# Last edge layer's table of query rows: one scatter of a four-row record a column in place of three, and pair gathers that start one row further on

## Chip, cores and metric

The kernel runs on one core of a Trainium2 chip. The metric is the device time of one launch in microseconds (us); the median of the runs counts.

## What is computed

Four layers on 6250 nodes of 256 features: a graph attention layer, a mixture of experts, a second graph attention layer with edge attributes, and a slice attention. The change is in the third. Its reference, cut to what matters (H = 8 heads of C = 32, 100000 edges sorted by target):

```python
q = (x @ Wq + bq).reshape(n, H, C)
k = (x @ Wk + bk).reshape(n, H, C)
v = (x @ Wv + bv).reshape(n, H, C)
e = (edge_attr @ We).reshape(-1, H, C)
k_j = k[src] + e
v_j = v[src] + e
q_i = q[dst]
alpha = jnp.sum(q_i * k_j, axis=-1) / jnp.sqrt(jnp.float32(C))
amax = jax.ops.segment_max(alpha, dst, num_segments=n)
ex = jnp.exp(alpha - amax[dst])
alpha = ex / denom[dst]
out = jax.ops.segment_sum(v_j * alpha[:, :, None], dst, num_segments=n)
out = out.reshape(n, HC) + x @ Ws + bs
```

`q_i = q[dst]` needs one row of q for each edge. Since the edges are sorted by target, two neighbouring edges need either the same row twice, or the rows of two targets that follow one another among the targets that have edges (their ranks).

## The kernel before

The program is a row of stages (`build`), each a block in which every engine has its own instruction list; a stage ends when all five engines have finished it, a barrier passes, its semaphores are cleared, and a second barrier passes. Two stages matter here, with an empty one between them.

**`layer1_tables` (L2000 to L2257).** Nodes lie on 128 partitions, 49 columns each, handled in 7 groups of 7 columns. For a group VectorE normalizes 7 columns (`normalize_group`), TensorE turns them (L2228) and ScalarE copies them out of PSUM (L2194); for a column TensorE makes query, key, value and skip rows in eight matmuls of 512 columns (L2246), VectorE adds the biases in four instructions (L2170 to L2173), and ScalarE writes the scaled query row twice side by side into the tile `twice` (L2212). GpSimd (POOL) then scatters it into the table `c.q` in HBM, in which a target of rank r owns the four rows 4r+1 to 4r+4:

```python
pool.indirect_dma_start(pairs, at_slot(0, i), twice[...], None)          # 2 KB: rows 4r+2 and 4r+3
for n in range(1, 3):
    pool.indirect_dma_start(c.q, at_slot(n, i), twice[:, g % 2, j, 0, :], None)   # 1 KB each: rows 4r+4 and 4r+1
```

So 3 scatters a column, 147 in all. The first and last row of the table, which no target owns, are zeroed by SyncE (SP, L2045 and L2046). The 28 gathers at L2067, ahead of the scatters in POOL's list, fetch expert outputs of the last 14 columns, which VectorE adds during group 0. Where groups meet, VectorE adds the skip rows to x (L2180, 2 us) and normalizes the group after the next, ahead of its first bias addition; TensorE can do two columns meanwhile, since the PSUM tile `psO` has two buffers. Buffers of `qrow` and `twice` come free over `q_free` and `twice_free`; the latter needs all scatters of the group before to be issued and those of two groups before to be landed. When all groups are done, VectorE marks the segments of the edges and makes `c.q_of`, the pair index of each two edges (`segments_of_edges`, L2137 to L2152). SP stores the key and value rows of each group (L2052), and the stage waits for all stores and scatters.

**`order_attributes`** sorts edge attributes where edges come unsorted. Here they come sorted; every engine only passes its barriers, and POOL and SP read a flag and jump.

**`edge_pass` (L1023 to L1252).** 98 blocks of 8 edges on 128 partitions. For a block POOL issues 8 gathers of key and value rows (L1111, 2 KB a partition) and 4 gathers of query pairs (L1118, 2 KB), SP loads edge attributes (L1077, L1078) and stores the states (L1084). TensorE turns the attributes and adds keys (L1239, L1249, L1250). VectorE forms the products, the maxima, the weights and a running sum, in a fixed chain of instructions a block (L1140 to L1176). Queries, keys, values and attributes have two buffers.

Of the kernel before, what the change touches and what calls it, by code (L numbers as in the profile page):

```python
# [6 lines left out]
I32 = mybir.dt.int32  # L7
ALU = mybir.AluOpType
# [3 lines left out]
P = 128  # L12
N, D = 6250, 256
# [5 lines left out]
T = 784  # L19
# [1006 lines left out]
def edge_pass(c):  # L1026
# [8 lines left out]
    with ExitStack() as s:  # L1035
# [66 lines left out]
        def _(pool):  # L1102
            pairs = c.q.rearrange("(r two) d -> r (two d)", two=2)
            for blk in range(NBLK):
# [11 lines left out]
                for m in range(B // 2):  # L1116
                    t = blk * B + 2 * m
                    pool.indirect_dma_start(q[:, u, m, :], None, pairs, bass.IndirectOffsetOnAxis(  # L1118
                        ap=c.q_of[:, t // 2:t // 2 + 1], axis=0)).then_inc(gq[u], 16)
# [879 lines left out]
def layer1_tables(c):  # L1999
# [5 lines left out]
    with ExitStack() as s:  # L2005
# [6 lines left out]
        start, slots = sb("start", [P, NI], I32), sb("slots", [P, 3, NI], I32)  # L2012
# [3 lines left out]
        qrow, kvrow, srow = sb("qrow", [P, 2, GT, D]), sb("kvrow", [P, 2, GT, 2 * D]), sb("srow", [P, GT, D])  # L2016
        twice = sb("twice", [P, 2, GT, 2, D])
# [4 lines left out]
        starts_in, counted, summed, slots_made, numbered, twice_free, sc0, sc1, ends_in, turned = (sem(n) for n in (  # L2022
            "starts_in", "counted", "summed", "slots_made", "numbered", "twice_free", "sc0", "sc1", "ends_in", "turned"))
        q_biased, q_copied, q_free = sem("q_biased"), sem("q_copied"), sem("q_free")
# [6 lines left out]
        picked = [twice[:, 1], kvrow[:, 1].rearrange("p j (r d) -> p j r d", r=2)]  # L2031
# [3 lines left out]
        def _(sp):  # L2035
# [9 lines left out]
            sp.dma_start(c.q[0:1, :], c.zrow[0:1, 0:D]).then_inc(ends_in, 16)  # L2045
            sp.dma_start(c.q[4 * NI * P + 1:4 * NI * P + 2, :], c.zrow[0:1, 0:D]).then_inc(ends_in, 16)  # L2046
# [11 lines left out]
            sp.wait_ge(ends_in, 32)  # L2058
# [3 lines left out]
        def _(pool):  # L2062
# [6 lines left out]
            pairs = c.q.rearrange("(r two) d -> r (two d)", two=2)  # L2069
            at_slot = lambda n, i: bass.IndirectOffsetOnAxis(ap=slots[:, n, i:i + 1], axis=0)  # L2070
            pool.sem_inc(twice_free, 2)
            pool.wait_ge(slots_made, 1)
            for g in range(NG):
                for j in range(GT):
# [10 lines left out]
            pool.wait_ge(sc[(NG - 1) % 2], 3 * GT * 16 * ((NG - 1) // 2 + 1))  # L2085

        @block.vector
        def _(v):
# [3 lines left out]
            def rank_rows():  # L2092
# [39 lines left out]
            def segments_of_edges():  # L2132
# [27 lines left out]
            def step(g, par, ahead):  # L2160
# [26 lines left out]
        def _(act):  # L2187
# [14 lines left out]
            def step(g, par, ahead):  # L2202
                if ahead:
                    root_of(g + 1)
                act.wait_ge(twice_free, g + 1)
                if g == 1:
                    act.wait_ge(late_added, NI - late)
                for j in range(GT):
# [580 lines left out]
```

## Time and profile before

| what | us |
|---|---|
| runs, device time | 5677.88, 5679.74, 5673.19 |
| median of the runs | 5677.88 |
| profiled execution, first to last instruction (span) | 5673.3 |
| `layer1_tables`, first to last instruction | 3253.6 to 3496.1 |
| `edge_pass`, first to last instruction | 3503.7 to 5156.7 |

The profile records one execution: for each instruction its start and duration, and what ended the wait before it. The profiled execution's own time is not listed apart from its span; what lies around the span is therefore not known, and the span is 4.6 us below the median of the runs. Where the profile's tables have a share of DMA, that is the mean busy share of 16 DMA engines; PEclk is the granted clock of TensorE, 1.00 for 2.4 GHz and 0.50 for 1.2 GHz.

### The profile page before, as it was taken

Reading aid. Unit: us, or ns where it says so; the run is one execution under the profiler, and the core shown is the slowest. Engines: PE = TensorE matmul, PEld = TensorE weight load, DVE = VectorE, ACT = ScalarE, POOL = GpSimd, SP = SyncE. Lnnn points to the kernel's source line nnn. Section 1 sums busy time; section 2 is a strip of 40 time slices with the busy share of each in tenths; the row PEclk is TensorE's granted clock in tenths of the full one; section 3 lists DMA queues with packets and bytes.
Section 4 is the critical chain, followed back from the end, with each engine's and each line's share of the span. In section 5 each row is a group of like instructions: output and inputs, shape, how many; then the busy total and the mean of one; then the engine's idle time right before and its main releaser. Section 6 shows DMA issues by size and latency. Waiting matters only on the chain. (4 is left out here: it accounts for less than half of the span.)

```text
span 5673.3 us, 49658 instructions
## 1 busy us (share of the span) xinstructions
PE 2860.0 (50%) x13052; PEld 2232.1 (39%) x13052; DVE 3824.3 (67%) x6117; ACT 1441.9 (25%) x2526; POOL 3388.4 (60%) x3382
## 2 busy tenths in 40 slices
PE   7513200000000000015899986888888888884777
PEld 5412200000000000014677633777776777673456
DVE  7357778786454545546543464989899998995763
ACT  1113333332233333311222211222222222221320
POOL 0267777777777777753440276777777777773200
PEclk9655555555555555556799998999999999896888
DMA  3133344432363333323232355999999999993114
GB/s 101 36 84 108 107 130 148 130 104 83 103 220 110 109 110 109 110 87 124 93 124 68 107 191 191 317 319 323 319 319 321 319 323 318 323 318 113 67 47 148
DMA packets 290231, 961.79 MB, mean 170 GB/s; under 512 B 79248, under 2 KB 119831, under 8 KB 248468
## 3 DMA queue, kind: packets, MB, share of 16 engines
q0 software_dynamic: 171296, 483.60, 28.6%
q1 hardware_dynamic: 118788, 476.59, 24.9%
q8 instruction: 48, 0.79, 0.1%
q14 instruction: 99, 0.81, 0.0%
HBM read 626.03 MB, written 345.69 MB: 171 GB/s over the span
## 5 line engine op out<-in xcount | busy, mean ns | idle before, releaser
L1249 PE MATMUL e_psE<-e_we,e_eaT 128*128 128x256 f32 x3136 | 903.5, 415 | 279.3 <-DVE e_wv L1148 179.3
L1111 POOL DMA_INDIRECT e_kv<-kv,rec x784 | 875.7, 1117 | 266.3 <-issue 253.7
L779 POOL DMA_INDIRECT g_g<-t,rec x784 | 777.1, 991 | 254.0 <-issue 253.7
L779 POOL DMA_INDIRECT g_g<-t,dst_of x784 | 743.6, 949 | 259.3 <-issue 257.2
L1249 PEld LDWEIGHTS e_psE<-e_we,e_eaT 128*128 128x128 f32 x3136 | 649.4, 210 | 400.7 <-ACT e_eaT L1192 299.4
L1407 PE MATMUL j_psM<-ident,tail 128*128 128x128 f32 x32 | 7.2, 416 | 1149.0 <-PEq L53 1149.0
L1250 PE MATMUL e_psE<-e_kv,ident 128*128 128x256 f32 x1568 | 509.8, 409 | 0.0
L816 DVE TENSOR_TENSOR_SCAN g_wv<-g_fx,g_wv 128x2176 f32<-128x2176 f32 x98 | 459.0, 4684 | 0.2 <-issue 0.2
L1407 PEld LDWEIGHTS j_psM<-ident,tail 128*128 128x128 f32 x32 | 6.8, 322 | 1149.8 <-issue 1149.8
L1118 POOL DMA_INDIRECT e_q<-q,q_of x392 | 370.9, 946 | 119.7 <-issue 119.7
L956 ACT ACTIVATE g_st<-g_wv 128x2048 f32<-128x2048 f32 x98 | 375.9, 3836 | 0.0
L1176 DVE SCALAR_TENSOR_TENSOR e_st<-e_st,e_kept,e_wv 128x256 f32<-128x256 f32 x686 | 336.3, 490 | 57.4 <-issue 9.7
L811 DVE TENSOR_TENSOR g_wv<-g_g,g_fx 128x2048 f32<-128x2048 f32 x98 | 370.4, 3780 | 3.3 <-issue 0.4
L1250 PEld LDWEIGHTS e_psE<-e_kv,ident 128*128 128x128 f32 x1568 | 325.7, 208 | 52.8
L791 DVE TENSOR_TENSOR g_at<-g_g,g_ar_b 128x64 f32<-128x64 f32 x49 | 13.1, 268 | 450.3 <-DMA g_g<-t,dst_of 450.3
L1147 DVE TENSOR_TENSOR e_q<-e_psE,e_q 128x1024 f32<-128x1024 f32 x196 | 239.3, 1221 | 17.9 <-issue 14.7
L1166 DVE TENSOR_TENSOR e_wv<-e_wv,e_cw 128x2048 f32<-128x2048 f32 x98 | 224.6, 2292 | 32.4 <-ACT e_cw L1207 32.4
L966 PE MATMUL g_spare<-g_ol,g_oh 128*128 128x64 bf16 x784 | 105.0, 303 | 269.4 <-DVE g_ol L119 267.4
L1148 DVE TENSOR_TENSOR e_wv<-e_kv,e_psE 128x1024 f32<-128x1024 f32 x196 | 237.2, 1210 | 0.0
L1151 DVE TENSOR_REDUCE e_at<-e_q 128x64 f32<-128x2048 f32 x98 | 224.2, 2288 | 13.3
L940 ACT ACTIVATE g_cw<-g_ex 128x128 f32<-128x128 f32 x98 | 30.3, 309 | 791.5 <-DVE g_ex L804 791.5
L977 PE MATMUL g_spare<-ident,g_ka 128*128 128x128 f32 x56 | 13.7, 426 | 430.6 <-DVE g_ka L580 430.6
(519 smaller groups left out, 6620.8 us busy)
## 6 DMA issues: line engine op xcount, KB each, us to landing
state<-e_st SPq DMA_DIRECT2D x98, 1088.0 KB, 6.2
e_ea<-in_edge_attr SPq DMA_DIRECT2D x98, 896.0 KB, 9.8
state_f<-g_st SPq DMA_DIRECT2D x49, 1088.0 KB, 4.4
state_b<-g_st SPq DMA_DIRECT2D x49, 1088.0 KB, 4.3
m_work<-xs SPq DMA_DIRECT2D x119, 128.0 KB, 2.3
ys<-m_work SPq DMA_DIRECT2D x119, 128.0 KB, 1.7
xs<-g_ta SPq DMA_DIRECT2D x28, 512.0 KB
g_g<-t,rec POOLq DMA_INDIRECT x784
```

The source lines that it names most:

```text
L779: pool.indirect_dma_start(g[:, u, j, :], None, tab, bass.IndirectOffsetOnAxis(ap=at_, axis=0)).then_inc(gat[u], 16)
L811: tt(msg(wv[:, :, 1:G1].rearrange("p n b -> p b n")), msg(g[:, u, :, 0:P]), pw[:, :, 0:G].rearrange("p h b -> p b h").unsqueeze(3).to_broa ...
L816: nc.vector.tensor_tensor_scan(flat(wv[:]), flat(fx), flat(wv[:]), 0.0, ALU.mult, ALU.add).then_inc(std, 1)
L956: nc.scalar.activation(st[:, u, :, 0:P], wv[:, :, 1:G1].rearrange("p n b -> p b n"), ACT.Copy).then_inc(act_st, 1)
L1111: pool.indirect_dma_start(kv[:, u, b, :], None, c.kv, bass.IndirectOffsetOnAxis(ap=c.rec[:, t, 1:2], axis=0)).then_inc(gkv[u][b // 4], 16)
L1118: pool.indirect_dma_start(q[:, u, m, :], None, pairs, bass.IndirectOffsetOnAxis(ap=c.q_of[:, t // 2:t // 2 + 1], axis=0)).then_inc(gq[u], 16)
L1147: tt(q4, quad, q4, ALU.mult)
L1148: tt(wv[:, 4 * half:4 * half + 4, :], v4, quad.rearrange("p (j n) -> p j n", j=4), ALU.add).then_inc(ed, 2)
L1166: tt(weighed, weighed, cw[:, :, 1:B1].rearrange("p h b -> p b h").unsqueeze(3).to_broadcast([P, B, H, C]), ALU.mult)
L1176: last = nc.vector.scalar_tensor_tensor(out=st[:, u, b, 0:D], in0=st[:, u, b - 1, 0:D] if b else before[:], scalar=kept[:, u, b:b + 1], in ...
L1249: nc.tensor.matmul(half, eaT[:, m, j, k, :], we[:, k, :], start=(k == 0), stop=False)
L1250: last = nc.tensor.matmul(half, c.ident[:], kv[:, u, 2 * m + j, 0:D], start=False, stop=True)
```

## The change

A rank r now owns the rows 4r to 4r+3. The tile `fourfold` holds four equal rows, ScalarE's copy writes all four, and one scatter a column writes them as one record of 4 KB. The scatter's index is the rank itself, so the three index computations become one copy. Pairs are gathered one row further on (`element_offset=D`): record k of a pair is rows 2k+1 and 2k+2, so equal targets take k = 2r (rows 4r+1, 4r+2), unequal ones k = 2r+1 (4r+3 and 4r+4). `c.q_of` is computed to fit. The table has no end rows, so SP's two stores of zeros go. `qrow` has one buffer in place of two, and VectorE waits for ScalarE's copy of the same column of the group before in place of `q_free`.

```diff
@@ edge_pass, gpsimd
                     pool.indirect_dma_start(q[:, u, m, :], None, pairs, bass.IndirectOffsetOnAxis(
-                        ap=c.q_of[:, t // 2:t // 2 + 1], axis=0)).then_inc(gq[u], 16)
+                        ap=c.q_of[:, t // 2:t // 2 + 1], axis=0), element_offset=D).then_inc(gq[u], 16)
@@ layer1_tables, tiles
-        qrow, kvrow, srow = sb("qrow", [P, 2, GT, D]), sb("kvrow", [P, 2, GT, 2 * D]), sb("srow", [P, GT, D])
-        twice = sb("twice", [P, 2, GT, 2, D])
+        qrow, kvrow, srow = sb("qrow", [P, GT, D]), sb("kvrow", [P, 2, GT, 2 * D]), sb("srow", [P, GT, D])
+        fourfold = sb("fourfold", [P, 2, GT, 4, D])
@@ sync
-            sp.dma_start(c.q[0:1, :], c.zrow[0:1, 0:D]).then_inc(ends_in, 16)
-            sp.dma_start(c.q[4 * NI * P + 1:4 * NI * P + 2, :], c.zrow[0:1, 0:D]).then_inc(ends_in, 16)
...
-            sp.wait_ge(ends_in, 32)
@@ gpsimd
                     i = g * GT + j
-                    pool.indirect_dma_start(pairs, at_slot(0, i), twice[:, g % 2, j, :, :].rearrange("p r d -> p (r d)"),
-                                            None).then_inc(sc[g % 2], 16)
-                    for n in range(1, 3):
-                        pool.indirect_dma_start(c.q, at_slot(n, i), twice[:, g % 2, j, 0, :], None).then_inc(sc[g % 2], 16)
+                    pool.indirect_dma_start(quads, bass.IndirectOffsetOnAxis(ap=slots[:, i:i + 1], axis=0),
+                                            fourfold[:, g % 2, j, :, :].rearrange("p r d -> p (r d)"), None).then_inc(sc[g % 2], 16)
                 if g:
-                    pool.wait_ge(sc[1 - g % 2], 3 * GT * 16 * ((g - 1) // 2 + 1))
-                    pool.sem_inc(twice_free, 1)
+                    pool.wait_ge(sc[1 - g % 2], GT * 16 * ((g - 1) // 2 + 1))
+                    pool.sem_inc(copies_free, 1)
@@ vector
-                ts(slots[:, 0, :], rank[:], 2.0, 1.0, ALU.mult, ALU.add)
-                ts(slots[:, 1, :], rank[:], 4.0, 4.0, ALU.mult, ALU.add)
-                ts(slots[:, 2, :], rank[:], 4.0, 1.0, ALU.mult, ALU.add).then_inc(slots_made, 1)
+                nc.vector.tensor_copy(slots[:], rank[:]).then_inc(slots_made, 1)
...
-                ts(count, count, offs[:, 0:1], 2.0, ALU.add, ALU.mult)
-                v.drain()
-                tt(c.q_of[:], count[:, 0:T:2], c.same[:, 1:T:2], ALU.subtract)
+                ts(count, count, offs[:, 0:1], -0.5, ALU.add, ALU.add)
+                v.drain()
+                nc.vector.scalar_tensor_tensor(out=c.q_of[:], in0=count[:, 0:T:2], scalar=2.0, in1=c.same[:, 1:T:2],
+                                               op0=ALU.mult, op1=ALU.subtract)
...
-                v.wait_ge(q_free, g + 1)
                 for j in range(GT):
                     v.wait_ge(mm, g * GT + j + 1)
                     o = psO[j % 2]
-                    tt(qrow[:, par, j, :], o[0][:, 0:D], ball[:, 0:D], ALU.add).then_inc(q_biased, 1)
+                    if g:
+                        v.wait_ge(q_copied, (g - 1) * GT + j + 1)
+                    tt(qrow[:, j, :], o[0][:, 0:D], ball[:, 0:D], ALU.add).then_inc(q_biased, 1)
@@ scalar
-                    last = nc.scalar.activation(twice[:, par, j, :, :], qrow[:, par, j, :].unsqueeze(1).to_broadcast([P, 2, D]),
+                    last = nc.scalar.activation(fourfold[:, par, j, :, :], qrow[:, j, :].unsqueeze(1).to_broadcast([P, 4, D]),
                                                 ACT.Copy, scale=float(C) ** -0.5)
                     last.then_inc(q_copied, 1)
-                act.wait_ge(q_copied, (g + 1) * GT)
-                act.sem_inc(q_free, 1)
```

POOL's list of `layer1_tables` before, from the gathers of expert outputs (`ys`) to the scatters of the first columns (`q` is the table in HBM, `q_slots` the indices):

```order
L2063 IOTA q_ids 128x49
L2067 DMA q_twice<-ys,slot 128x256 x14
L2067 DMA q_kvrow<-ys,slot 128x256 x14
L2078 DMA q<-q_twice,q_slots 12545x512 [waits h_const_made,h_t_wt]
L2081 DMA q<-q_twice,q_slots 25090x256 x2
L2078 DMA q<-q_twice,q_slots 12545x512 [waits h_t_wt]
L2081 DMA q<-q_twice,q_slots 25090x256 x2
```

The same place, and what follows it, with the change:

```order
L2060 IOTA q_ids 128x49
L2064 DMA q_fourfold<-ys,slot 128x256 x14
L2064 DMA q_kvrow<-ys,slot 128x256 x14
L2074 DMA q<-q_fourfold,q_slots 6272x1024 [waits h_const_made,h_logits_kept]
L2074 DMA q<-q_fourfold,q_slots 6272x1024 [waits h_logits_kept] x13
L2074 DMA q<-q_fourfold,q_slots 6272x1024 [waits h_w_in,h_logits_kept]
```

Each column's wait for ScalarE's copy is now followed by one scatter in place of three.

At the end of the stage before, the last scatters and the way to `edge_pass` over the jumped stage (L999 to L1002):

```order
L2078 DMA q<-q_twice,q_slots 12545x512 [waits h_t_wt]
L2081 DMA q<-q_twice,q_slots 25090x256 x2
L2005 UNCONDITIONAL_BRANCH [waits h_cleared,h_w_in]
L52 ISA [waits barrier_Pool_Activation_PE_DVE_SP_gather]
L999 UNCONDITIONAL_BRANCH [waits barrier_Pool_Activation_PE_DVE_SP_gather]
L60 TENSOR_LOAD flag
```

With the change one scatter (L2074) stands where these three do, and the rest of this piece stays.

## Rows read from the trace of the kernel before

**Rows 1.** Waits of `edge_pass`, 3600 to 5100 us: us in total, times, longest.
```profile
PE e_psE L1249 <- DVE e_wv L1148: 171.7, 46, 4.5
DVE e_wv L1166 <- ACT e_cw L1207: 30.0, 91, 0.3
DVE e_q L1147 <- issue: 13.8, 89, 0.2
```

**Rows 2.** Stretches of `edge_pass`: busy us of each engine.
```profile
core 0: us, PE busy (x) PEld busy (x) DVE busy (x) ACT busy (x) POOL busy (x), PEclk, DMA share, GB/s
...
4200.00:4500.00 300.00, 247.59 (x1158) 213.28 (x1157) 270.60 (x380) 72.20 (x207) 230.69 (x218) 0.91 1.00 321
```

**Rows 3.** Groups of POOL's instructions by form, whole program: busy, mean ns, idle before.
```profile
L2081 POOL DMA_INDIRECT q<-q_twice,q_slots x98 | 101.0, 1031 | 30.6 <-issue 26.2 <-ACT q_twice L2212 4.4
L2078 POOL DMA_INDIRECT q<-q_twice,q_slots x49 | 51.5, 1051 | 23.3 <-issue 13.1 <-ACT q_twice L2212 10.2
```

**Rows 4.** Timeline of TensorE, one column of group 5 and all of group 6.
```profile
3449.87 0.38 PE L2228 MATMUL q_psT<-ident,q_xln 128*128 128x128 f32 x2
...
3453.52 0.60 PE L2228 MATMUL q_psT<-ident,q_xln 128*128 128x128 f32 x4
3455.29 24.27 PE L2246 MATMUL q_psO<-q_w,q_xT 128*128 128x512 f32 x56 [1.17 <-DVE q_srow L2173]
```

**Rows 5.** Timeline of TensorE after VectorE's normalization, in the third and fourth group.
```profile
3341.37 5.40 PE L2246 MATMUL q_psO<-q_w,q_xT 128*128 128x512 f32 x8 [2.41 <-DVE q_srow L2173]
...
3372.71 3.70 PE L2246 MATMUL q_psO<-q_w,q_xT 128*128 128x512 f32 x8 [2.41 <-DVE q_srow L2173]
```

**Rows 6.** Timeline of ScalarE where groups 5 and 6 meet.
```profile
3454.22 0.62 ACT L2212 ACTIVATE q_twice<-q_qrow 128x512 f32<-128x512 f32 x1
3454.74 0.38 ACT L2194 ACTIVATE q_xT<-q_psT 128x256 f32<-128x256 f32 x1
...
3480.06 0.63 ACT L2212 ACTIVATE q_twice<-q_qrow 128x512 f32<-128x512 f32 x1 [2.80 <-DVE q_qrow L2170]
```

**Rows 7.** Timeline at the end of `layer1_tables`.
```profile
3481.09 0.34 SPq L2052 DMA_DIRECT2D kv<-q_kvrow  x1
...
3491.48 0.57 DVE L2152 TENSOR_TENSOR q_of<-q_xln,same 128x392 int32<-128x392 f32 x1
...
3495.14 0.96 POOL L2081 DMA_INDIRECT q<-q_twice,q_slots  x1 [0.30 <-issue]
3503.71 0.40 SPq L1061 DMA_DIRECT2D e_we<-in_L_gnn_We  x1
```

**Rows 8.** Stretches from POOL's last scatter to the first instruction of `edge_pass`.
```profile
3496.10:3497.10 1.00, 0.00 (x0) 0.00 (x0) 0.00 (x0) 0.00 (x0) 0.00 (x0) 0.50 0.36 131
3497.10:3503.70 6.60, 0.00 (x0) 0.00 (x0) 0.00 (x0) 0.00 (x0) 0.00 (x0) 0.50 0.00 0
```

**Rows 9.** DMA issues, 3240 to 3510 us: KB each, median us from issue to landing.
```profile
kv<-q_kvrow SPq DMA_DIRECT2D x7, 1792.0 KB, 6.4
q<-q_twice,q_slots POOLq DMA_INDIRECT x147, 2.7
```

**Rows 10.** Timeline where the stage before the experts ends with VectorE.
```profile
2646.35 0.42 DVE L1541 SCALAR_TENSOR_TENSOR x<-c_tmp,x 128x256 f32<-128x256 f32 x1
2647.62 0.38 SPq L1694 DMA_DIRECT2D m_wg<-in_L_ffn_Wg  x1
```

**Rows 11.** Groups of ScalarE's copies by form: busy, mean ns of one.
```profile
L956 ACT ACTIVATE g_st<-g_wv 128x2048 f32<-128x2048 f32 x98 | 375.9, 3836 | 0.0
L2212 ACT ACTIVATE q_twice<-q_qrow 128x512 f32<-128x512 f32 x49 | 30.6, 625 | 25.6 <-DVE q_qrow L2170 25.6
L2194 ACT ACTIVATE q_xT<-q_psT 128x256 f32<-128x256 f32 x49 | 18.8, 383 | 114.4 <-PE q_psT L2228 114.3
```

**Rows 12.** Timeline of the index computations on VectorE.
```profile
3268.44 0.18 DVE L2118 TENSOR_SCALAR q_slots<-q_rank 128x49 int32<-128x49 f32 x1
3268.53 0.18 DVE L2119 TENSOR_SCALAR q_slots<-q_rank 128x49 int32<-128x49 f32 x1
```

More of the change, by code:

```diff
@@ L2011, in layer1_tables @@
         xln, xT = sb("xln", [P, GT, D]), sb("xT", [P, 2, 2, GT * P])
-        start, slots = sb("start", [P, NI], I32), sb("slots", [P, 3, NI], I32)
+        start, slots = sb("start", [P, NI], I32), sb("slots", [P, NI], I32)
         some, rank, zeros, ids = (sb(n, [P, NI]) for n in ("some", "rank", "zeros", "ids"))
@@ L2021, in layer1_tables @@
             "ld", "vin", "root", "xr", "tr", "tc", "mm", "od", "rows", "st0", "st1"))
-        starts_in, counted, summed, slots_made, numbered, twice_free, sc0, sc1, ends_in, turned = (sem(n) for n in (
-            "starts_in", "counted", "summed", "slots_made", "numbered", "twice_free", "sc0", "sc1", "ends_in", "turned"))
-        q_biased, q_copied, q_free = sem("q_biased"), sem("q_copied"), sem("q_free")
+        starts_in, counted, summed, slots_made, numbered, copies_free, sc0, sc1, turned = (sem(n) for n in (
+            "starts_in", "counted", "summed", "slots_made", "numbered", "copies_free", "sc0", "sc1", "turned"))
+        q_biased, q_copied = sem("q_biased"), sem("q_copied")
         sc = [sc0, sc1]
@@ L2030, in layer1_tables @@
         late_in = [sem(f"late_in{n}") for n in range(GT)]
-        picked = [twice[:, 1], kvrow[:, 1].rearrange("p j (r d) -> p j r d", r=2)]
+        picked = [fourfold[:, 1, :, 0:2], kvrow[:, 1].rearrange("p j (r d) -> p j r d", r=2)]
         block = s.enter_context(nc.Block())
@@ L2068, in _ @@
                         ap=c.slot[:, late + n, k:k + 1], axis=0)).then_inc(late_in[n // 2], 16)
-            pairs = c.q.rearrange("(r two) d -> r (two d)", two=2)
-            at_slot = lambda n, i: bass.IndirectOffsetOnAxis(ap=slots[:, n, i:i + 1], axis=0)
-            pool.sem_inc(twice_free, 2)
+            quads = c.q.rearrange("(r four) d -> r (four d)", four=4)
+            pool.sem_inc(copies_free, 2)
             pool.wait_ge(slots_made, 1)
@@ L2077, in _ @@
                     i = g * GT + j
-                    pool.indirect_dma_start(pairs, at_slot(0, i), twice[:, g % 2, j, :, :].rearrange("p r d -> p (r d)"),
-                                            None).then_inc(sc[g % 2], 16)
-                    for n in range(1, 3):
-                        pool.indirect_dma_start(c.q, at_slot(n, i), twice[:, g % 2, j, 0, :], None).then_inc(sc[g % 2], 16)
+                    pool.indirect_dma_start(quads, bass.IndirectOffsetOnAxis(ap=slots[:, i:i + 1], axis=0),
+                                            fourfold[:, g % 2, j, :, :].rearrange("p r d -> p (r d)"), None).then_inc(sc[g % 2], 16)
                 if g:
-                    pool.wait_ge(sc[1 - g % 2], 3 * GT * 16 * ((g - 1) // 2 + 1))
-                    pool.sem_inc(twice_free, 1)
-            pool.wait_ge(sc[(NG - 1) % 2], 3 * GT * 16 * ((NG - 1) // 2 + 1))
+                    pool.wait_ge(sc[1 - g % 2], GT * 16 * ((g - 1) // 2 + 1))
+                    pool.sem_inc(copies_free, 1)
+            pool.wait_ge(sc[(NG - 1) % 2], GT * 16 * ((NG - 1) // 2 + 1))
         @block.vector
@@ L2204, in step @@
                     root_of(g + 1)
-                act.wait_ge(twice_free, g + 1)
+                act.wait_ge(copies_free, g + 1)
                 if g == 1:
@@ L2211, in step @@
                     act.wait_ge(q_biased, g * GT + j + 1)
-                    last = nc.scalar.activation(twice[:, par, j, :, :], qrow[:, par, j, :].unsqueeze(1).to_broadcast([P, 2, D]),
+                    last = nc.scalar.activation(fourfold[:, par, j, :, :], qrow[:, j, :].unsqueeze(1).to_broadcast([P, 4, D]),
                                                 ACT.Copy, scale=float(C) ** -0.5)
                     last.then_inc(q_copied, 1)
-                act.wait_ge(q_copied, (g + 1) * GT)
-                act.sem_inc(q_free, 1)
-            act.sem_inc(q_free, 2)
             each_group(prepare, step)
@@ L2725, in build @@
     c.xs, c.ys = ([dram(f"{w}{n}", ((TILES[n + 1] - TILES[n]) * P, D)) for n in range(len(PARTS))] for w in ("xs", "ys"))
-    c.kv, c.q = dram("kv", (NI * P, 512)), dram("q", (4 * NI * P + 2, D))
+    c.kv, c.q = dram("kv", (NI * P, 512)), dram("q", (4 * NI * P, D))
     with ExitStack() as s:
```

## Prediction

> **What bounds the kernel now.** I read the stages in the order of their size, and in each asked which wait ends last. `edge_pass` comes first, because the change alters where its gathers read. Its waits name VectorE: TensorE waits for VectorE's reading of PSUM, 171.7 us of the stretch, while VectorE's own longest waits are 30.0 us for ScalarE's exponential, 0.33 us a block, and 13.8 us of issue; no wait of VectorE for a gather is among them [rows 1]. It is busy 270.6 of 300 us, and the rest is drains between dependent instructions [rows 2]. So a block lasts as long as VectorE's chain, about 16.5 us (98 blocks in 1653 us, start-up included; its 91 waits for ScalarE fall in 1500 us [rows 1]). The same rows hold a warning: the DMA share is 1.00 at 321 GB/s. The DMA engines are never seen idle, though nobody waits for them.
>
> In `layer1_tables` POOL looks like the bound: 147 scatters, busy 152.5 us, in a stretch of some 206 us (3289.9 to 3496.1), nearly all the rest being issue gaps of 0.3 us [rows 3]. But TensorE has no more room. A column takes it 3.66 us (3449.87 to 3453.52), and in the last group, with no transposes between, 24.27 us for seven columns, 3.44 each after the first [rows 4]. POOL needs 3 x (0.96 + 0.30) = 3.78 us a column, taking the 0.96 us of an undisturbed scatter [rows 7]. Two engines go at almost one pace; POOL loses 0.12 us a column and recovers it where groups meet, since there TensorE stands still for 2.4 us until VectorE has normalized the next group [rows 5]. POOL waited for ScalarE 14.6 us in all [rows 3]. So only what POOL still has to do when TensorE and VectorE have finished lies on the path. That is the tail of the stage: VectorE ends with `q_of` at 3491.48 + 0.57 = 3492.05, POOL's last scatter ends at 3495.14 + 0.96 = 3496.10, and `edge_pass` starts at 3503.71 [rows 7].
>
> **The change part by part.**
>
> *Scatters.* 98 of 147 go, and with them 98 x 1.26 = 123 us of POOL. Hidden beside TensorE is all of that but the tail. For the 4 KB record the trace has no row. From below: 0.96 us, which is what both a 2 KB and a 1 KB record take in these rows, size not showing. From above: three times the present instruction, 3 x 1.26 = 3.78 us, which is today's pace and no gain. I take 0.96, the nearest. After the last copy POOL then ends about 1.3 us later, and the record lands some 2.7 us after its issue [rows 9], near 3486.
>
> *The end of the stage.* Before, it was set by the last scatter's landing: 3495.14 + 2.7 = 3497.8, which fits the traffic that ends near 3497.1 [rows 8]. From there to 3503.71 pass 5.9 us with no work in any engine: two stage ends, their barriers, and the jumped stage with its flag. These stay. A stage end where VectorE is last costs 0.85 us by itself (2646.77 to 2647.62) [rows 10], so the 5.9 us are not all explained by barriers; I come back to that as a rival. After, the last of the stage is VectorE at 3492.05; the last store of key and value rows lands at 3481.09 + 6.4 = 3487.5 [rows 7, 9], ahead of it. So the end moves from 3497.8 to 3492.05: **-5.8 us**. Were the landing counted from the instruction's end, it would be -6.7.
>
> *ScalarE's copy.* It writes 1024 columns in place of 512. The rows for 256 and 512 columns are 383 and 625 ns [rows 11], 242 ns for each 256 more, hence 1.11 us; from above, the 1.87 ns a column of the 128x2048 copy gives 1.92 us. With the 0.38 us transposed copy a column is 1.5 us (2.3 at most) of ScalarE against 3.44 us, so it is hidden, except once: where groups meet the last transposed copy stands behind a query copy (3454.22, then 3454.74) and TensorE's next matmul behind it (3455.29) [rows 4, 6]. That start moves by 0.49 us. At five of the six meetings TensorE stands for 2.4 us two columns later anyway [rows 5], which swallows it. At the last meeting, without normalization, it stays: **+0.5 us** (+1.3 by the upper price).
>
> *Index computations.* Two of three instructions go, issued 0.09 us apart [rows 12], ahead of the first matmul: **-0.2 us**. `q_of` has as many instructions as before.
>
> *Waits, buffers, SP.* The wait for `q_copied` of the group before is met some 25 us earlier, so the single `qrow` costs nothing; behind that wait on VectorE stand the bias additions TensorE needs, and a late wait would show there. `copies_free` now comes earlier, POOL being less behind. SP's two stores of zeros lie 30 us ahead of its first store of rows. Nothing.
>
> *Gathers of pairs.* The same number of instructions, descriptors and bytes, starting at an odd 1 KB row. VectorE hides what they take; the price of a start that is not on a 2 KB boundary is not in the trace. I take zero, with a bound below as a rival.
>
> Sum: -5.8 + 0.5 - 0.2 = **-5.5 us**. Against the profiled span that is 5673.3 - 5.5 = 5667.8; the median of the runs is 4.6 us above that span, so 5677.9 - 5.5 = **5672.4**.
>
> A rule of the Trainium skill beside the landing: "DMA: Bandwidth & Descriptors", in the section on the anatomy of a DMA from GpSimd, gives a fixed cost of about 2.0 us plus bytes at 436 GB/s. For the last 128 KB that would be 2.3 us against the 2.7 us of the rows, and the gain 5.4 us before the two small terms in place of 5.8; the sum goes by the row.
>
> **The rivals.**
>
> *The clock comes back (chance 0.13).* After the wait of 2.4 us TensorE's first column took 5.40 us in one group, 3.70 in the next, with the same wait ahead of it [rows 5]: 1.7 us paid for the 1.2 GHz level. Of the five such columns four took 5.40. If ScalarE's later copy shortens this standstill by 0.5 us and the clock stays up in each of the four slow groups, 4 x 1.7 = 6.8 us more are gained: 5665.6. Against it: the 0.5 us only move from this standstill to the one before it, so the sum of idle time is the same.
>
> *The long tail was POOL's (0.09).* If the 5.9 us after the landing come with a scatter as the last work, and VectorE as last pays only 0.85 us [rows 10], the start of `edge_pass` moves from 3503.7 to about 3493.2: -10.5 us, 5667.4. Against it: the jumped stage lies in the one interval and not in the other.
>
> *The 4 KB record takes POOL three times as long (0.05).* Then POOL ends as today, and the time is 5678.
>
> *Gathers at the odd row are slower (0.13): the one on the other side.* Place: the 392 gathers in `edge_pass`. They move 1.05 of the 5.3 MB of a block (4 of 256 KB, beside 2.1 MB of keys and values, 1.0 of attributes and 1.1 of states), 20%. With a DMA share of 1.00 [rows 2] there may be no room at all: each per cent that they take longer is then 0.2% of 16.5 us, 0.033 us a block, 3.3 us over 98 blocks. The 5.5 us gained are used up at 1.7%, and at 5% the kernel is slower by more than 0.2%. At 10%, which I take as the case, it is +33 - 5.5: 5705. For it: the full share. Against it: VectorE never waits for them, and only some 6% of pairs (at most 6250 changes of target among 50000 pairs, and half of those) read across a 4 KB record. The Trainium skill, "DMA: Bandwidth & Descriptors", on how a descriptor splits into transactions, says that a start on a multiple of 256 B costs nothing extra; a 1 KB row is one. No row here shows that.
>
> **How the numbers follow.** The forecast keeps 0.60. Its own range is 5667 to 5678: both ends of the landing, the upper copy price, and the 3 us by which the runs shown lie to either side. The predicted time is its 5672.4. The whole range, 5662 to 5682, takes in the clock, the long tail and the slow record; left out are the slow gathers, 0.13, and the rest of the clock's case. 0.2%, about what a measurement of this kernel can tell from no change, is 11.4 us: faster means under 5666.5. That holds for most of the clock's case and part of the long tail's: 0.17. Slower, over 5689.2, is the gathers' case: 0.13. Within: 0.70.
>
> **What would show it.** In the profile after: 49 scatters near 0.96 us with waits for ScalarE between; the copy near 1.1 us; VectorE's `q_of` near 3492.3 as the last work of the stage; `edge_pass` starting 5 to 6 us earlier and lasting 1653 us still. The forecast is wrong if TensorE's 3.66 us a column changes, if the gap ahead of `edge_pass` shrinks or grows, or if VectorE in `edge_pass` shows waits for `e_q`.

## The result, and the profile after

The changed kernel takes 5650.24 us, median of four runs (5645.79 to 5653.78), against 5675.72 (median of four, 5673.19 to 5679.74) for the kernel before; the ratio is 0.9953 (95% interval 0.9942 to 0.9965). So it is faster by 25.5 us, 0.45%. I had forecast 5672.4 and "no change"; the time lies outside my range. The profiled spans, 5673.3 and 5649.4 us, divide so:

| from, to | before | after | difference |
|---|---|---|---|
| start to `layer1_tables` | 3253.6 | 3250.2 | -3.4 |
| first instruction of `layer1_tables` to that of `edge_pass` | 250.1 | 243.4 | -6.7 |
| first instruction of `edge_pass` to that of the next stage | 1657.6 | 1640.8 | **-16.8** |
| the rest | 512.0 | 515.0 | +3.0 |

The first and last rows are code that was not changed; I come back to them. `layer1_tables` did what was forecast. `edge_pass`, which I had costed at zero, made most of the difference.

**The tables.** Groups by form, whole program (busy, mean ns, idle before), after:

```profile
L2074 POOL DMA_INDIRECT q<-q_fourfold,q_slots x49 | 55.2, 1127 | 139.1 <-ACT q_fourfold L2206 136.1 <-issue 3.0
L2206 ACT ACTIVATE q_fourfold<-q_qrow 128x1024 f32<-128x1024 f32 x49 | 51.6, 1052 | 20.7 <-DVE q_qrow L2164 20.7
```

POOL's 49 scatters are busy 55.2 us against 152.5 [rows 3], and POOL waits 136.1 us for ScalarE. Its waiting is the gain that does not reach the end: a column still takes TensorE 3.66 us (3442.74 to 3446.40 in the rows below). The timeline where the stage ends, the TensorE rows being those of a column of group 5 and of group 6:

```profile
3442.74 3.60 PE L2237 MATMUL q_psO<-q_w,q_xT 128*128 128x512 f32 x8
3446.18 0.38 PE L2219 MATMUL q_psT<-ident,q_xln 128*128 128x128 f32 x2
3446.40 3.60 PE L2237 MATMUL q_psO<-q_w,q_xT 128*128 128x512 f32 x8
3449.84 0.60 PE L2219 MATMUL q_psT<-ident,q_xln 128*128 128x128 f32 x4
3451.91 24.30 PE L2237 MATMUL q_psO<-q_w,q_xT 128*128 128x512 f32 x56 [1.47 <-ACT q_xT L2188]
...
3475.12 0.95 POOL L2074 DMA_INDIRECT q<-q_fourfold,q_slots  x1 [2.48 <-ACT q_fourfold L2206]
3478.55 2.09 POOL L2074 DMA_INDIRECT q<-q_fourfold,q_slots  x1 [2.48 <-ACT q_fourfold L2206]
...
3487.95 0.57 DVE L2144 SCALAR_TENSOR_TENSOR q_of<-q_xln,same 128x392 int32<-128x392 f32 x1
3493.64 0.39 SPq L1061 DMA_DIRECT2D e_we<-in_L_gnn_We  x1
```

VectorE is last, at 3488.52, and `edge_pass` starts 5.12 us later. Before, it started 11.66 us after VectorE's end [rows 7]. An undisturbed scatter of 4 KB records takes 0.95 us like one of 1 or 2 KB.

**The edge pass.** The view I had read, its waits and stretches, shows nothing that would be 17 us. Waits of 3600 to 5100 us, and the stretch from 4200, after:

```profile
PE e_psE L1249 <- DVE e_wv L1148: 137.7, 46, 4.2
DVE e_wv L1166 <- ACT e_cw L1207: 29.9, 91, 0.3
4200.00:4500.00 300.00, 249.03 (x1165) 214.52 (x1165) 270.79 (x383) 72.42 (x208) 232.98 (x221) 0.91 1.01 323
```

Against [rows 1, 2] VectorE is as busy as it was and waits as long. What differs is the duration of one small instruction, seen only when its two kinds of blocks are told apart. Groups by form, 3600 to 5100 us, of the kernel before and then of the changed one:

```profile
L1140 DVE COPY e_at<-e_mt 128x8 f32<-128x8 f32 x90 | 26.2, 291 | 3.3
```

```profile
L1140 DVE COPY e_at<-e_mt 128x8 f32<-128x8 f32 x92 | 15.8, 171 | 5.8
```

The mean of 291 ns is 0.17 us in every odd block and 0.41 in every even one. The timeline of the kernel before, VectorE and then POOL, across such an even start (u = 0, behind the loop's branch):

```profile
4224.51 0.49 DVE L1176 SCALAR_TENSOR_TENSOR e_st<-e_st,e_kept,e_wv 128x256 f32<-128x256 f32 x1
4225.18 3.33 DVE L1176 SCALAR_TENSOR_TENSOR e_st<-e_st,e_kept,e_wv 128x256 f32<-128x256 f32 x6 [0.19 <-issue]
4228.59 0.41 DVE L1140 COPY e_at<-e_mt 128x8 f32<-128x8 f32 x1
...
4228.05 0.95 POOL L1111 DMA_INDIRECT e_kv<-kv,rec  x1 [0.30 <-issue]
```

and of the changed kernel:

```profile
4240.04 3.87 DVE L1176 SCALAR_TENSOR_TENSOR e_st<-e_st,e_kept,e_wv 128x256 f32<-128x256 f32 x7
4244.04 0.17 DVE L1140 COPY e_at<-e_mt 128x8 f32<-128x8 f32 x1
...
4243.59 1.14 POOL L1111 DMA_INDIRECT e_kv<-kv,rec  x1 [0.30 <-issue]
```

Two things are to be seen. (A drain is an instruction that holds VectorE's list until the instruction ahead of it has ended; one stands between each two state sums, L1176.) Before, the copy and POOL's gather end together: 4228.59 + 0.41 and 4228.05 + 0.95 are both 4229.00. The copy comes when the gather is 0.54 us old, and waits for it; that it is the gather it waits for is tested below, in e7. After, it comes at 0.45 us, takes 0.17, and the gather takes 0.19 us longer instead. And before, the seven state sums are broken in one place by 0.19 us of issue; from one instruction to the next that is 0.118 us more than in its neighbours. After, they are not.

Over the pass the copies' waits in the kernel before sum to 11.4 us, and 48 times 0.118 us is 5.7: together 17.1, for the 16.8 us to be explained. The Trainium skill, "SBUF — State Buffer", in the section on its two separate sides, states that VectorE and GpSimd share a pair of ports as an exclusive lock, held by whoever starts first, and that a copy of 4-byte elements from SBUF to SBUF takes it. By that rule, the trace agrees in part: one of the two pays, 0.24 us the copy or 0.19 us the gather. But the gather is the first to start in both cases, by 0.54 or by 0.45 us, and in the second it is the one that pays; so it can't hold the ports from its recorded start on, as the rule taken by itself would have it. What the rule doesn't say either is why the copy should come 0.09 us earlier after this change. No part of the change is in VectorE's loop.

### The profile page after: what moved, and what is told of

The parts are those of the page before. It is cut to its first block and busy times, and to the rows that moved or that the text cites. A ratio compares the mean times of both kernels' runs of the same rounds, so it can differ in the third digit from the quotient of the medians.

```text
span 5649.4 us, 49583 instructions
## 1 busy us (share of the span) xinstructions
PE 2856.7 (51%) x13052; PEld 2230.7 (39%) x13052; DVE 3808.5 (67%) x6115; ACT 1462.3 (26%) x2526; POOL 3287.9 (58%) x3284
## 5 line engine op out<-in xcount | busy, mean ns | idle before, releaser
L1176 DVE SCALAR_TENSOR_TENSOR e_st<-e_st,e_kept,e_wv 128x256 f32<-128x256 f32 x686 | 335.4, 489 | 51.3
L1147 DVE TENSOR_TENSOR e_q<-e_psE,e_q 128x1024 f32<-128x1024 f32 x196 | 239.2, 1221 | 17.1 <-issue 14.9
L1166 DVE TENSOR_TENSOR e_wv<-e_wv,e_cw 128x2048 f32<-128x2048 f32 x98 | 224.7, 2293 | 32.3 <-ACT e_cw L1207 32.3
## 6 DMA issues: line engine op xcount, KB each, us to landing
xs<-g_ta SPq DMA_DIRECT2D x28, 512.0 KB
```

The costliest lines, as they stand in the source:

```text
L1147: tt(q4, quad, q4, ALU.mult)
L1166: tt(weighed, weighed, cw[:, :, 1:B1].rearrange("p h b -> p b h").unsqueeze(3).to_broadcast([P, B, H, C]), ALU.mult)
L1176: last = nc.vector.scalar_tensor_tensor(out=st[:, u, b, 0:D], in0=st[:, u, b - 1, 0:D] if b else before[:], scalar=kept[:, u, b:b + 1], in ...
```

## The experiments

All runs were timed beside the kernel before, whose median on those chips was 5677.5 to 5678.9 us. "A pair" is the median time of two blocks of `edge_pass`, from one even L1140 to the next: 33.14 us in the kernel before, 32.80 in the changed one.

**Is it the gathers, or where VectorE's loop stands?** VectorE's list as built has 6210 instructions before and 6244 after. In its list of `layer1_tables` semaphore instructions go from 7 to 43: the seven that waited for `q_free` are replaced by 42 for `q_copied`, one ahead of each column's first bias addition from the second group on, and one for a matmul. Two index instructions go, which leaves 34 more, all ahead of the loop.

```diff
@@ e1_before_34_drains (kernel before; 30 on the changed one in e3; on the one before 4 in e4, 1 in e5, 2 in e6, 128 in e11, 256 in e12)
             v.sem_inc(ed, 4)
+            for _ in range(34):
+                v.drain()
             with v.Fori(0, NBLK // U) as i:
@@ e2_even_rows (changed kernel)
-                        ap=c.q_of[:, t // 2:t // 2 + 1], axis=0), element_offset=D).then_inc(gq[u], 16)
+                        ap=c.q_of[:, t // 2:t // 2 + 1], axis=0)).then_inc(gq[u], 16)
...
-                                            fourfold[:, g % 2, j, :, :].rearrange("p r d -> p (r d)"), None).then_inc(sc[g % 2], 16)
+                                            fourfold[:, g % 2, j, :, :].rearrange("p r d -> p (r d)"), None, element_offset=D).then_inc(sc[g % 2], 16)
...
-                ts(count, count, offs[:, 0:1], -0.5, ALU.add, ALU.add)
+                ts(count, count, offs[:, 0:1], 0.0, ALU.add, ALU.add)
```

In e2 SyncE also zeroes the four end rows that the table has again.

> The kernel before, with 34 drains added to VectorE's list ahead of its loop in edge_pass, where VectorE waits for the first gathers anyway. This brings the loop to the place in VectorE's list that it has in the changed kernel; POOL, the table and the gathers stay as before. Theory A (the place of the loop in VectorE's list decides two small stalls): L1140 takes 0.175 us in every block, the period of two blocks falls from 33.20 to 32.84 us, edge_pass from 1657.7 to about 1641, the time from 5675.7 to about 5659. Theory B (the gathers at the odd row, or the new table, made edge_pass shorter): the period stays 33.20 us and the time 5675 to 5677.

> The changed kernel with one scatter of 4 KB a column, but each record one row further on (rank r owns rows 4r+1 to 4r+4), so that the scatter's records are not aligned to 4 KB and the pairs are gathered from even rows, as before the change. VectorE's list has as many instructions as in the changed kernel. Theory A (place of VectorE's loop): everything as in the changed kernel, edge_pass 1641, the time about 5650. Theory B (the gathers' row or the record's alignment made edge_pass shorter): the period of two blocks goes back to 33.20 us, edge_pass to 1657, the time to 5667.

> The changed kernel with 30 drains ahead of VectorE's loop in edge_pass. With the 34 instructions that the change itself adds to VectorE's list that makes 64. Theory A, with places that repeat every 64 instructions: both stalls come back, L1140 takes 0.415 us in every second block, the period of two blocks is 33.20 us again, the time 5667. Theory A with another spacing (128 or 256), or theory B: the period stays 32.84 and the time 5650 to 5652.

> The kernel before with only 4 drains ahead of VectorE's loop in edge_pass. Theory A with places 64 instructions apart, one of them three instructions behind the loop's start in the kernel before: four instructions move it out of the loop, so the 0.24 us of L1140 go (11.8 us over 49 pairs of blocks), while the other place stays in the loop and costs 0 to 0.12 us a pair of blocks: the time is 5658 to 5664. If the whole shift of 34 is needed, or the stalls have nothing to do with the list: 5675.

| run | time, us | ratio to before | a pair | even L1140 |
|---|---|---|---|---|
| before + 34 drains | 5658.96 | 0.9968 (0.9956 to 0.9979) | 32.81 | 0.175 |
| changed, even rows | 5654.56 | 0.9963 (0.9950 to 0.9975) | 32.82 | 0.175 |
| changed + 30 drains | 5655.99 | 0.9963 (0.9950 to 0.9975) | 32.81 | 0.175 |
| before + 4 drains | 5662.24 | 0.9979 (0.9969 to 0.9989) | 32.81 | 0.175 |

Theory B is out: with the gathers of before (even rows) `edge_pass` stays short, and with nothing but drains added the kernel before gains 18.6 us, its `edge_pass` lasting 1641.8 us in place of 1657.6. The rival of slow gathers at the odd row falls with it, 32.82 against 32.80. The third run refuted my spacing of 64. The time of the fourth fell into the range I had given for it, but by luck: the place at the head of the loop on which that range rested isn't there, as e5 and e6 show below. Comparing, in all loops, the time from the start of each instruction to that of the next gave theory C. At one place of the list, behind instruction 5816 as built (counted from 0) in every one of these programs, the next instruction comes 0.114 us late. In the changed kernel and in e1 it lies behind a state sum, in e3 behind the copy, in e4 behind the scan L1172 with the first state sum and a drain after it; in the kernel before it lies behind a drain. Behind a state sum (L1176) the drain that follows covers it, as its own time shrinks from 0.49 to 0.38 us, and in e4 the drain's from 0.66 to 0.54; behind the drain nothing does.

**One drain or two.** The sharpest test of that, and of the race for the port, is a step of one instruction:

> The kernel before with one drain more ahead of VectorE's loop in edge_pass. From the runs so far: at one fixed place of VectorE's list the next instruction is handed over 0.114 us late. In the kernel before this place lies behind the drain of the second state sum of the second block, where nothing covers it; behind a state sum the drain covers it. One instruction more puts it behind the second state sum itself. Theory C (the uncovered 0.118 us makes L1140 come too late, so that it has to wait until POOL's gather, issued 0.53 us earlier, ends): both 0.118 and 0.24 us go, the median period of two blocks falls from 33.14 to 32.80 us, the time is about 5660. Theory D (L1140 waits because that place, or a second one, lies at the head of the loop): one instruction moves nothing away from there, the period stays 33.0 to 33.14 us and the time 5670 to 5677.

> The kernel before with two drains more ahead of the same loop. The late place now lies behind the drain of the first state sum of the second block: uncovered again, and still between the port's release by L1166 and L1140. Theory C: L1140 takes 0.415 us again in every second block, the period of two blocks is 33.14 us as in the kernel before, the time 5675 to 5678, although four drains and one drain gained. Theory D (head of the loop): as with one or with four drains, one of 33.14 or 32.80, with nothing that singles out two from one and four.

> The kernel before with VectorE's copy at L1140 written as the maximum of the tile with itself, an instruction of two inputs; list and places are unchanged. Theory C with the port: only the copy takes the port that POOL needs to write a gather's descriptors. L1140 takes 0.17 to 0.20 us in every block, and the gather of POOL beside it 0.95 us and not 1.14; the uncovered 0.118 us stays: period of two blocks 32.90 us, time about 5665. If two inputs take the port as well, or if L1140 is late for a reason of the list: 0.41 us in every second block, 33.14 us, 5677. The Trainium skill, SBUF, in the section on its two separate sides, says that GpSimd and VectorE share a pair of ports, that whichever starts first holds it to the end of its instruction, and that two SBUF inputs block only a GpSimd operation that reads SBUF.

```diff
@@ e7_before_copy_as_two_inputs
-                    copy(at[:, :, 0], mt[:, :, B])
+                    tt(at[:, :, 0], mt[:, :, B], mt[:, :, B], ALU.max)
```

| run | time, us | ratio to before | a pair | even L1140 |
|---|---|---|---|---|
| before + 1 drain | 5662.36 | 0.9973 (0.9963 to 0.9982) | 32.81 | 0.176 |
| before + 2 drains | 5679.13 | 1.0002 (0.9992 to 1.0011) | 33.13 | 0.410 |
| copy with two inputs | 5668.03 | 0.9983 (0.9973 to 0.9993) | 32.90 | 0.175 |

One drain is worth 15.6 us, the second gives it all back. In the timeline of the kernel with two drains the gap has moved one state sum forward and L1140 waits again:

```profile
4223.71 0.46 DVE L1178 SCALAR_TENSOR_TENSOR e_st<-e_before,e_kept,e_wv 128x256 f32<-128x256 f32 x1
4224.36 3.89 DVE L1178 SCALAR_TENSOR_TENSOR e_st<-e_st,e_kept,e_wv 128x256 f32<-128x256 f32 x7 [0.19 <-issue]
4228.32 0.41 DVE L1142 COPY e_at<-e_mt 128x8 f32<-128x8 f32 x1
```

With the copy written as an instruction of two inputs the gap stays and the wait goes, at the same age of the gather (4223.47, so 0.54 us):

```profile
4220.60 3.33 DVE L1176 SCALAR_TENSOR_TENSOR e_st<-e_st,e_kept,e_wv 128x256 f32<-128x256 f32 x6 [0.19 <-issue]
4224.01 0.17 DVE L1140 TENSOR_TENSOR e_at<-e_mt 128x8 f32<-128x8 f32 x1
...
4223.47 0.95 POOL L1111 DMA_INDIRECT e_kv<-kv,rec  x1 [0.30 <-issue]
```

That separates the two costs: 33.14 - 32.90 = 0.24 us of port, 32.90 - 32.80 = 0.10 us of gap. Only half of what I expected of POOL came true: in the odd blocks, where the instruction comes when the gather is 0.24 us old, it still holds POOL up (1.14 us).

**Three attempts on POOL's side, none of which told anything about the race.** The drains and what replaced them stand ahead of the seventh gather of keys and values.

> The kernel before with two drains in POOL's list ahead of the seventh gather of keys and values of each block, so that the eighth, which stands beside L1140, starts 0.1 us later or more; VectorE's list is unchanged. Theory C: the copy is now first at the port, L1140 takes 0.175 us in every block, the period of two blocks is 32.90 us (the uncovered 0.118 us stays), the time about 5665. POOL's later gathers cost nothing, since each block has 1.0 to 1.4 us in which POOL waits for the port behind L1166. Theory D, or a cause in VectorE's list alone: L1140 0.415 us, 33.14 us, 5677. If POOL has no room: the period grows by the drains, above 33.2 us.

> The kernel before with six semaphore instructions in POOL's list ahead of the seventh gather of keys and values of each block, in place of the two drains, each of which held POOL until its gathers had landed. VectorE's list is unchanged. Theory C: the eighth gather starts 0.1 us later or more against L1140, which is then first at the port: L1140 0.175 us in every block, two blocks 32.90 us (the uncovered 0.118 us stays), time about 5665. If L1140's wait has its cause in VectorE's own list: 0.415 us, 33.14 us, 5677.

> The kernel before with one memset of one column a block in POOL's list ahead of the seventh gather of keys and values; the six semaphore instructions had moved POOL by nothing. VectorE's list is unchanged. Theory C: the eighth gather starts later against L1140 by what the memset takes (0.07 us or more), so that it is 0.45 us old or less when L1140 comes, as in the changed kernel: L1140 0.175 us in every block, two blocks 32.90 us (the uncovered 0.118 us stays), time about 5665. If L1140's wait has its cause in VectorE's own list: 0.415 us, 33.14 us, 5677. A memset that itself holds VectorE up, or that delays the gathers by more than the 1.0 to 1.4 us of room, would show as a period above 33.2 us.

```diff
@@ e8_before_pool_later; in e8b six times pool.wait_ge(used, blk - U + 1) and c.alone(pool); in e8c a memset of idle[:, blk:blk + 1]
                 for b in range(B):
                     t = blk * B + b
+                    if b == 6:
+                        pool.drain()
+                        pool.drain()
                     pool.indirect_dma_start(kv[:, u, b, :], None, c.kv, ...)
```

Two drains gave 6407.27 us, ratio 1.1281 (1.1262 to 1.1299): each pair of drains holds POOL 5.1 to 10.4 us (6.72 in the rows below), until the gathers ahead of it have landed: in all 87 pauses between 3600 and 5700 us POOL's next gather starts 1.33 us after the last landing. This is the outcome "no room", and then some.

```profile
4258.94 0.95 POOL L1114 DMA_INDIRECT e_kv<-kv,rec  x1 [0.30 <-issue]
4266.61 0.95 POOL L1114 DMA_INDIRECT e_kv<-kv,rec  x1 [6.72 <-issue]
```

Six semaphore instructions (5678.83 us, ratio 0.9999, 0.9990 to 1.0009) and a memset (5678.36, 1.0002, 0.9993 to 1.0012) moved POOL by nothing; both fit into the 0.30 us that pass between gathers anyway:

```profile
4244.89 0.95 POOL L1114 DMA_INDIRECT e_kv<-kv,rec  x1 [0.30 <-issue]
4245.83 0.11 POOL L1113 MEMSET e_idle<- 128x1 f32 x1
4246.14 0.95 POOL L1114 DMA_INDIRECT e_kv<-kv,rec  x1 [0.19 <-issue]
```

**How far apart are the late places?**

> The kernel before with 128 drains ahead of VectorE's loop in edge_pass: how far apart the late places are. 64 more instructions than before (34 of the change and 30 drains) left only the one place already known. If the places are 128 apart, this kernel is as before the change: L1140 0.415 us in every second block, 33.14 us for two blocks, about 5675. If they are further apart, no late place lies in the loop: 32.80 us, about 5660.

> The kernel before with 256 drains ahead of the same loop. If the late places are 128 or 256 instructions apart: as before the change, L1140 0.415 us in every second block, 33.14 us for two blocks, about 5675 and up to 10 us more if the drains outlast the first gathers. If they are further apart: 32.80 us. The Trainium skill, Runtime: NRT & Kernel Launch, in the section on instruction fetch, speaks of blocks of 256 instructions and of a crossing that is mostly hidden.

Both have the gap where the kernel before has it, behind the same drain, so the late place is met again 128 and 256 instructions on. The times, one run each, are 5668.37 and 5669.94 us: about halfway. The same program now loses the race in some blocks and wins it in others. The gap is a little smaller here (0.10 us). Two even blocks of the kernel with 128 drains, each copy with the gather beside it:

```profile
4223.82 0.17 DVE L1142 COPY e_at<-e_mt 128x8 f32<-128x8 f32 x1
...
4223.29 1.20 POOL L1111 DMA_INDIRECT e_kv<-kv,rec  x1 [0.30 <-issue]
```

```profile
4289.78 0.40 DVE L1142 COPY e_at<-e_mt 128x8 f32<-128x8 f32 x1
...
4289.24 0.95 POOL L1111 DMA_INDIRECT e_kv<-kv,rec  x1 [0.30 <-issue]
```

At 0.53 us after the gather's start the copy wins, at 0.54 it loses 0.24 us. Of the 44 even blocks from the tenth on 22 were won, all at 0.526 to 0.532 us, and 22 lost, at 0.530 to 0.543. Pairs last 32.88 or 33.11 us, nothing between. (With 256 drains the copy wins at 0.506 to 0.516 us and loses at 0.513 to 0.527, and 12 of its 22 won blocks leave the gather at 0.95 us.) VectorE's list is the same in both kinds of block, so this shows what the three attempts on POOL could not: the wait isn't set by where the copy stands in the list, but, within one program, by when it comes. The age at which it turns isn't the same in all programs, though: in the kernel before the copies come at 0.519 to 0.539 us and all 44 lose, where with 128 drains ages up to 0.532 win. So something that these ages don't show has a part in it, and the smaller gap alone isn't shown to be what puts the copy on the edge.

The Trainium skill, "Runtime: NRT & Kernel Launch", in the section on instruction fetch, speaks of blocks of 256 instructions whose crossing is mostly hidden. The runs show a late place that is met again 128 instructions on, worth 0.10 to 0.12 us. Crossings 256 apart would not give that; what the late place is, no run here shows.

**The term of the tables, undone.** In place of the one scatter (there is one drain ahead of VectorE's loop as well, which with the one index instruction more leaves the late place behind a state sum):

```diff
+                ts(slots[:, 0, :], rank[:], 2.0, 0.0, ALU.mult, ALU.add)
+                ts(slots[:, 1, :], rank[:], 4.0, 0.0, ALU.mult, ALU.add).then_inc(slots_made, 1)
...
+                    pool.indirect_dma_start(c.q.rearrange("(r two) d -> r (two d)", two=2), bass.IndirectOffsetOnAxis(ap=slots[:, 0, i:i + 1], axis=0),
+                                            fourfold[:, g % 2, j, 0:2, :].rearrange("p r d -> p (r d)"), None).then_inc(sc[g % 2], 16)
+                    for n in range(2, 4):
+                        pool.indirect_dma_start(c.q, bass.IndirectOffsetOnAxis(ap=slots[:, 1, i:i + 1], axis=0),
+                                                fourfold[:, g % 2, j, n, :], None, element_offset=n * D).then_inc(sc[g % 2], 16)
```

> The changed kernel with three scatters a column again (one of 2 KB and two of 1 KB, to the same four rows), all else as changed: ScalarE's copy of four rows, the gathers at the odd row. One index instruction and one drain more on VectorE, which leave the late place of its loop covered. The prediction's term for the end of the stage: from the first instruction of layer1_tables to the first of edge_pass 250 us as before the change, not 243.4, since POOL is last again; edge_pass stays at 32.80 us for two blocks; time about 6 to 7 us over the changed kernel, 5656 to 5660. If the gain of the stage came from ScalarE's copy, the waits or the index work, it stays 243 to 245 us and the time at 5650 to 5653.

Measured: 5660.33 us, ratio 0.9968 (0.9956 to 0.9980), and 249.4 us from `layer1_tables` to `edge_pass`; a pair stays at 32.81 us. POOL's last scatter is issued at 3493.78, and the next stage starts at 3502.34:

```profile
3491.39 0.57 DVE L2150 SCALAR_TENSOR_TENSOR q_of<-q_xln,same 128x392 int32<-128x392 f32 x1
...
3493.78 0.96 POOL L2079 DMA_INDIRECT q<-q_fourfold,q_slots  x1 [0.30 <-issue]
3502.34 0.39 SPq L1061 DMA_DIRECT2D e_we<-in_L_gnn_We  x1
```

So six of the 6.7 us come back with the number of scatters: 5.3 behind VectorE's end, which `edge_pass` now follows by 10.39 us in place of 5.12, and 0.7 ahead of it. A single profile doesn't tell the size more closely. Over the twelve profiles with three scatters a column this stretch lasted 249.1 to 253.5 us, of which 10.4 (four profiles) or 11.6 to 11.7 (eight) came behind VectorE's end; over the four with one scatter it lasted 239.5 to 243.8, and 5.1 behind VectorE's end in each. The two kinds don't overlap. From the end of POOL's last scatter to the next stage pass 7.60 us here and 7.61 in the kernel before [rows 7], against 5.12 from VectorE's end in the changed one; the 2.5 us between fit a landing, counted from the instruction's end.

**A version to beat both.** The four copies, each in this way:

```diff
@@ e10_after_copies_as_two_inputs
-                copy(cw[:, 1, :, 0], den[:, :, G])
+                tt(cw[:, 1, :, 0], den[:, :, G], den[:, :, G], ALU.max)
```

> The changed kernel with VectorE's small copies beside gathers written as the maximum of a tile with itself: L1140 in edge_pass, and three in the first layer's aggregation (L789, L803, L814), whose copies wait up to some 15 us in all over their usual 0.17 us in the trace of the changed kernel. Theory C: in edge_pass nothing changes for VectorE (32.80 us for two blocks), POOL's gather beside L1140 takes 0.95 us in place of 1.14; in the first layer the long copies go and up to 15 us of its 2040 us, as far as they lay on the path: time 5638 to 5650. If the copies had waited for something else, or ran beside slack: 5650 as the changed kernel.

The long copies are gone from the first layer's trace, but its aggregation lasts 2112 us from its first row to its last, as in the changed kernel (2113). The time, 5652.10 us (ratio 0.9955, 0.9941 to 0.9968), is that of the changed kernel. Those copies waited beside slack; what they took over their usual time was busy time, not path. The other half of what I expected failed too: POOL's gather beside L1140 still takes 1.14 us, with the instruction of two inputs coming at 0.45 us. So two inputs spare VectorE's wait in e7, but not POOL's in any run where the instruction came early in the gather.

## Why the prediction missed

- **What bounds `edge_pass`: right.** VectorE's chain, no wait for gathers, before or after. But "so a block lasts as long as VectorE's chain, about 16.5 us", and then "lasting 1653 us still", took the chain as a constant. It was 33.14 us a pair with 0.34 us in it that were no work. My even mean over blocks hid it, and so did the idle column: a wait for the port is counted as busy time of the copy.
- **The step that failed** is "The wait for `q_copied` of the group before is met some 25 us earlier, so the single `qrow` costs nothing." As a wait that is true. As 42 instructions it isn't nothing: less the seven semaphore instructions and the two index instructions that go, and with the one that comes, they move VectorE's later loop by 34 places, which covers the gap of 0.118 us (5.7 us over the pass), and the copy then comes in time for the port (11.4 us). I had counted instructions on POOL and never on VectorE.
- **The end of the stage: right in kind, -5.8 forecast.** VectorE's end to `edge_pass` went from 11.66 to 5.12 us, -6.5. Mis-sized was the landing; the other reading of it, counted from the instruction's end, -6.7, was the better one here.
- **ScalarE's copy and the index work**, forecast +0.5 and -0.2: the copy takes 1.05 us (1.11 forecast), the standstill at the last meeting grew from 1.77 us [rows 4] to 2.07, +0.3. From the stage's start to VectorE's end it is -0.1 in all.
- **The 4 KB record and gathers at the odd row: zero, as taken.** By the Trainium skill, "DMA: Bandwidth & Descriptors", a start on a multiple of 256 B costs nothing extra; e2 agrees, a pair being 32.82 us on even rows and 32.80 on odd ones.
- **The rivals.** The clock did not come back in the profiled run: of the five columns behind a standstill, now 1.9 to 2.8 us, four again took 5.40 us (granted clock 0.68) and one 3.70 (1.00). But in e3 and e10, whose tables are those of the changed kernel, only two took 5.40 and three 3.70, which is 3.4 us less and fits their short `layer1_tables` (239.5 and 240.3 us). In all twelve profiles with three scatters four of the five were slow. Why it differs isn't shown, and the rival is open to that extent. The long tail of POOL was there, but as 2.5 us of landing. None of my cases contained what happened in `edge_pass`. A slip in the working of the slow gathers changes nothing: at 5% its own terms give 5 x 3.3 - 5.5 = 11.0 us, just under 0.2%, not more.
- **The two rows of unchanged code** stay unexplained in their sizes. Over the profiles of kernels that are equal up to there, `layer1_tables` started at 3249.9 to 3259.1 us, and what follows `edge_pass` lasted 511.0 to 518.7 us; -3.4 and +3.0 lie within that, and I read nothing into them.

Added up, -16.8 and -6.7 make 23.5 of the 25.5 us of the medians.

## What to carry to other kernels

A loop that runs a hundred times on the bounding engine should be read by kind of iteration, start to start, before its length is taken as given: equal instructions with two durations are a wait in disguise. When a change adds or removes instructions ahead of such a loop, on any engine that bounds a later stage, a difference of some 0.1 to 0.3 us an iteration can come from the shift alone; one spare drain ahead of the loop tells (15.6 us here, and a second took them back). And a small copy on VectorE beside a stream of gathers is cheaper as an instruction of two inputs, where its time is on the path: it saved 0.24 us in every second block in e7, and nothing in e10, off the path.

## What the hardware showed that I had not expected

- One place in VectorE's list hands over the next instruction 0.10 to 0.12 us late, in every iteration; it repeats 128 and 256 instructions on, and 64 on it does not. A drain after a long enough instruction covers it fully.
- Within one program the race between the copy and the gather is decided by some 0.01 us of the copy's start, 0.51 to 0.53 us into the gather, and losing costs 0.24 us at once. Where exactly it turns differs from program to program by some 0.02 us, and why isn't shown.
- VectorE holds POOL up without a semaphore between them: one gather of each block takes 1.96 to 2.33 us in place of 0.95. All 91 such gathers between 3600 and 5100 us start while L1166 (two inputs in SBUF, 2.29 us) runs, and end 0.81 to 0.83 us after it. In `layer1_tables` before, three of the last scatters took 2.81, 2.15 and 1.56 us beside VectorE's last addition of skip rows (L2180) and its work on the edges' segments. That this too is the port wasn't tested.
- A drain on POOL waits until its gathers have landed (5.1 to 10.4 us), while a memset of 0.11 us costs nothing between two gathers.
